# Opening four PSUM banks with a bias product, and reordering the first loads, in a two-layer network kernel

## The reference

```
h     = silu(noise_encoding(t) @ W1 + b1) @ W2 + b2          # t: one number per sequence
scale, shift = h @ Wsc + bsc, h @ Wsh + bsh
out   = silu(scale * LN(x) * gamma + beta ... + shift)       # LN over all 512 x 512 values of a sequence
out   = out @ W_in + b_in
out   = silu(scale * LN(out) ... + shift)
x2    = out @ W_out + b_out + x
r     = gelu(x2 @ Wi[e] + bi[e]) @ Wo[e] + bo[e] + x2        # e: one of 8 experts per sequence, hidden size 2048
y     = LN over channels (r) * gamma[e] + beta[e]
```

## Time and profile before

| | us |
|---|---|
| median of 3 runs (1773.46 to 1773.72) | 1773.62 |
| the profiled execution, own time | 1773.89 |
| its span | 1772.1 |

### The profile page before, as it was taken

One profiled execution on the slowest core, in us unless ns is written; L12 is line 12 of the kernel. 1 busy time (PEld: TensorE's weight loads), 2 busy tenths in 40 slices (PEclk: granted clock), 3 DMA queues, 4 the chain that ended last, 5 costly groups with the idle time before them and its releaser, 6 DMA issues.

```text
span 1772.1 us, 22301 instructions
## 1 busy us (share of the span) xinstructions
PE 1763.0 (99%) x7940; PEld 1454.7 (82%) x7940; DVE 1286.6 (73%) x2147; ACT 976.4 (55%) x1551; POOL 69.1 (4%) x138
## 2 busy tenths in 40 slices
PE   9999999999999999999999999999999999999998
PEld 6888888888888888888888888888888888888887
DVE  6876777767677777767777677677777777777576
ACT  4756554565545656456564555645556555565442
POOL 1000000000000000000000000000000000000000
PEclk9999999999999999999999999999999999999999
DMA  7332332323333233332332313333143332422321
GB/s 292 99 111 75 99 111 84 136 84 99 110 116 114 75 122 110 99 110 72 122 110 99 113 70 122 112 121 110 52 140 113 99 110 71 145 88 75 114 103 69
DMA packets 51906, 189.35 MB, mean 107 GB/s; under 512 B 10451, under 2 KB 14547, under 8 KB 35284
## 3 DMA queue, kind: packets, MB, share of 16 engines
q1 hardware_dynamic: 43156, 183.96, 29.8%
q10 hardware_dynamic: 8640, 3.97, 2.2%
HBM read 171.10 MB, written 16.81 MB: 106 GB/s over the span
## 4 chain that ended last, share of the span: by engine, by line
PE 98%; DMA 1%; SPq 1%; DVE 0%; issue 0%; ACT 0%; POOL 0%; DVEq 0%
PE out_acc L545 39%; PE hid_ps L545 39%; PE blk_ps L545 18%; DMA affine_sb<-in_affine 1%; SPq L364 1%; PE hid_ps L563 0%; PE blk_ps L563 0%; PE out_acc L590 0%; PE hid_ps L590 0%; PE hid_ps L587 0%; PE hid_ps L586 0%; PE blk_ps L586 0%; PE blk_ps L587 0%; PE blk_ps L590 0%; PE out_acc L586 0%
## 5 line engine op out<-in xcount | busy, mean ns | idle before, releaser
L545 PE MATMUL hid_ps<-x_hi,wi_hi 128*128 128x512 f32 x1020 | 397.1, 389 | 0.0
L545 PE MATMUL hid_ps<-x_hi,wi_lo 128*128 128x512 f32 x1020 | 397.1, 389 | 0.0
L545 PE MATMUL hid_ps<-x_lo,wi_hi 128*128 128x512 f32 x1020 | 397.1, 389 | 0.0
L545 PE MATMUL out_acc<-wo_lo,g_hi 128*128 128x512 f32 x1012 | 394.0, 389 | 0.0
L545 PE MATMUL out_acc<-wo_hi,g_hi 128*128 128x512 f32 x1012 | 394.0, 389 | 0.0
L545 PE MATMUL out_acc<-wo_hi,g_lo 128*128 128x512 f32 x1012 | 394.0, 389 | 0.0
L755 ACT ACTIVATE g_sb<-hid_ps,bi_sb 128x512 f32<-128x512 f32 x256 | 175.8, 687 | 311.2 <-PE hid_ps L545 310.9
L883 DVE TENSOR_TENSOR g_lo<-g_sb,g_hi 128x512 fp32r<-128x512 f32 x253 | 173.4, 685 | 189.4 <-ACT g_hi L759 187.7
L715 ACT ACTIVATE wo_hi<-stage 128x512 fp32r<-128x512 f32 x253 | 160.1, 633 | 172.5 <-PE out_acc L545 172.5
L545 PEld LDWEIGHTS hid_ps<-x_hi,wi_hi 128*128 128x128 f32 x1020 | 191.5, 188 | 39.9 <-DVE wi_lo L883 0.2
L545 PEld LDWEIGHTS hid_ps<-x_lo,wi_hi 128*128 128x128 f32 x1020 | 191.5, 188 | 39.6
(11 more groups left out here) (172 smaller groups left out, 1647.7 us busy)
## 6 DMA issues: line engine op xcount, KB each, us to landing
stage<-in_expert_w SPq DMA_DIRECT2D x128, 1024.0 KB, 4.9
x<-in_xT SPq DMA_DIRECT2D x15, 1024.0 KB, 7.3
out_y<-r_sb SPq DMA_DIRECT2D x15, 1024.0 KB, 5.1
rows<-in_expert_rows SPq DMA_DIRECT2D x16, 512.0 KB, 6.8
mv_all<-mv_dram ACTq DMA_DIRECT2D x30, 128.0 KB, 4.4
stage<-in_cond_w SPq DMA_DIRECT2D x4, 512.0 KB, 9.9
affine_sb<-in_affine SPq DMA_DIRECT2D x3, 512.0 KB, 10.2
x<-in_xT SPq DMA_DIRECT2D x4, 256.0 KB, 4.0
```

The costliest lines, as they stand in the source:

```text
L545: last = pe.matmul(dst, w[wp], xs[xp], start=start and i == 0, stop=stop and i == 2)
```

## The change

- SyncE no longer issues the head table and bias_rows: ScalarE's queue does, as its first two instructions. SyncE's order becomes x chunks 0 and 1, W1, x chunks 2 and 3, then as before.
- bias_rows gets b_in as a fourth part (8 KB in place of 6 KB, still one row).
- New `with_bias(m)`: a plain fp32 product of the row b_in (1 x 128) with a row of ones (1 x 512) that opens bank m of layer 1; `first_chunk(0, ...)` then adds onto it. With b_in in the banks, the addition into `bn`, its semaphore and `mean_less` go.
- TensorE's head: 9 products of zeros ahead of the sine in place of 7; `with_bias(0)` and `(1)`, then b2, then 2 zeros products after three statistics, in place of 9 zeros products; `with_bias(2)` in place of 2; `with_bias(3)` in place of 4; the second average is moved ahead of the W2 products; `scale_shift_bias(1)` stands between the W2 halves.
- VectorE: the turn of the W1 product is moved behind the four statistics and their aggregation; `h_lo_part(0, 0, 2)` is moved ahead of `affine(0, 0, 3)`.
- Other banks for the first average, the W1 and the W2 product.

```diff
...
@@ -238,14 +237,14 @@
 
         w1_raw = g_sb[:, 0, :]
         t_sb, cc, small_sb = head_sb[:, 0:B], head_sb[:, B:B + 3], head_sb[:, B + 3:]
-        b_in = small_sb[:, BIN:BIN + DC]
         w2_raw = stage[:, 0].rearrange("p a b n -> p (a b) n")
 
         def cond_raw(m):
             return stage[:, 1 + m // 2, m % 2].rearrange("p h (c n) -> p (h c) n", n=2 * P)
 
 
-        b2_row, bcond_row = (x_sb[1][0:1, a:b, :].rearrange("p c n -> p (c n)") for a, b in ((0, 1), (1, 3)))
+        b2_row, bcond_row, b_in_row = (x_sb[1][0:1, a:b, :].rearrange("p c n -> p (c n)")
+                                       for a, b in ((0, 1), (1, 3), (3, 4)))
         ones = rows[0:1, 0, :]
 
         w_raw = [r_sb, x2_turned]
...
@@ -348,8 +347,8 @@
             return cond_bank[m] if which else out_acc[m]
 
         cond_bank = hid_ps + blk_ps
-        stat_bank = [out_acc[0], blk_ps[1]]
-        m1_bank, m2_bank = out_acc[2], out_acc[3]
+        stat_bank = [blk_ps[1], blk_ps[1]]
+        m1_bank, m2_bank = hid_ps[1], blk_ps[0]
 
         def half(t, h):
 
@@ -372,11 +371,10 @@
             def load_w_in(c):
                 load(w_raw[0][:, c, :], W_in[c * P:(c + 1) * P, :], ld_w_in[c])
 
-            load(head_sb[:, :], head, ld_head)
-            load(w1_raw, W1, ld_w1)
             for c in range(DC):
                 load(x_sb[0][:, c, :], xT[0, c * P:(c + 1) * P, :], ld_first[c])
-            load(x_sb[1][0:1, 0:3, :].rearrange("p c n -> p (c n)"), bias_rows, ld_bias)
+                if c == 1:
+                    load(w1_raw, W1, ld_w1)
             for h in range(2):
                 load(half(w2_raw, h), W2[h], ld_w2[h])
             load_cond(0)
@@ -511,33 +509,41 @@
                     last = strips(m2_bank, m1[:, k, :], of_w(w2_raw[:, k, :]), P, stop=(k == DC - 1))
                 return last
 
+            def with_bias(m):
+
+                pe.matmul(block_bank(0, 0, m)[:, :], b_in_row[:, m * P:(m + 1) * P], ones,
+                          start=True, stop=False)
+
             pe.wait_ge(s_zero, 1)
-            keep_warm(hid_ps[0], 7)
+            keep_warm(hid_ps[0], 9)
             pe.wait_ge(ld_w1, 16)
             pe.wait_ge(s_pad, 1)
             pe.wait_ge(s_sin, 1)
             strips(m1_bank, enc_sin[:, :], of_w(w1_raw), P, start=True, stop=True).then_inc(s_mm1, 1)
-            keep_warm(hid_ps[0], 9)
             pe.wait_ge(s_ones, 1)
             pe.wait_ge(ld_bias, 16)
+            with_bias(0)
+            with_bias(1)
             strips(m2_bank, ones[:, 0:BLOCK], of_w(b2_row), P, start=True)
+            pe.wait_ge(s_bn, DC - 1)
+            keep_warm(hid_ps[0], 2)
             pe.wait_ge(s_average, 1)
             pe.wait_ge(s_mv, 1)
             average_of(0, 0, mv[:, 0, 0:1])
-            keep_warm(out_acc[1], 2)
+            with_bias(2)
+            pe.wait_ge(s_sq, 1)
+            average_of(0, 1, dev[:, 0, 1:2])
             pe.wait_ge(s_pad, 2)
             pe.wait_ge(s_m1, DC)
             w2_half(0)
-            keep_warm(out_acc[1], 2)
-            pe.wait_ge(s_sq, 1)
-            average_of(0, 1, dev[:, 0, 1:2])
+            scale_shift_bias(1)
             w2_half(1).then_inc(s_mm2, 1)
             scale_shift_bias(0)
             pe.wait_ge(s_m2, 1)
             scale_shift(0)
-            for c in range(1, DC):
-                scale_shift_bias(c)
-            keep_warm(out_acc[1], 4)
+            scale_shift_bias(2)
+            scale_shift_bias(3)
+            with_bias(3)
 
             def three(dst, w, xs, start=False, stop=False):
 
@@ -561,7 +567,7 @@
                     else:
                         pe.wait_ge(s_silu, DC * which + 1)
                 pe.matmul(block_bank(0, which, m)[:, HALVES[n]], w_raw[which][:, 0, m * P:(m + 1) * P],
-                          work[:, 0, HALVES[n]], start=(n == 0), stop=False)
+                          work[:, 0, HALVES[n]], start=(bool(which) and n == 0), stop=False)
 
             def first_products(which, m, c):
 
@@ -718,6 +724,8 @@
 
                 act.activation(table_use[:, :], cc[:, 0:1], function)
 
+            act.dma_start(head_sb[:, :], head).then_inc(ld_head, 16)
+            act.dma_start(x_sb[1][0:1, :, :].rearrange("p c n -> p (c n)"), bias_rows).then_inc(ld_bias, 16)
             act.wait_ge(s_enc, 8)
             act.activation(enc_sin[:, 0:B], enc[:, 3, :], ACT.Sin).then_inc(s_sin, 1)
             load_table(ACT.Silu)
@@ -902,11 +910,6 @@
                 dve.bn_stats(bn[:, m, :], src).then_inc(s_bn, 1)
                 if m == DC - 1:
                     dve.wait_ge(s_bn, DC * (turn + 1))
-                    if (b, which) == (0, 1):
-                        means = bn[:, :, 1:6:3]
-                        dve.tensor_tensor(means, means, b_in.unsqueeze(2).to_broadcast([P, DC, 2]), ALU.add) \
-                           .then_inc(s_bnbias, 1)
-                        dve.wait_ge(s_bnbias, 1)
                     dve.bn_aggr(mv[:, which, :], bn[:, :, :]).then_inc(s_mv, 1)
 
             def totals(b, which):
@@ -926,11 +929,7 @@
                 dve.wait_ge(s_avg, 2 * which + 1)
                 dve.tensor_tensor(dev[:, which, 0:1], mv[:, which, 0:1], bank[:, 0:1], ALU.subtract) \
                    .then_inc(s_dev, 1)
-                if which:
-                    dve.tensor_tensor(mean_less[:, :], bank[:, 0:1].to_broadcast([P, DC]), b_in, ALU.subtract) \
-                       .then_inc(s_mean0, 1)
-                else:
-                    dve.tensor_copy(mean(0, which), bank[:, 0:1]).then_inc(s_mean0, 1)
+                dve.tensor_copy(mean(0, which), bank[:, 0:1]).then_inc(s_mean0, 1)
                 dve.wait_ge(s_dev, which + 1)
                 dve.scalar_tensor_tensor(out=dev[:, which, 1:2], in0=dev[:, which, 0:1],
                                          scalar=dev[:, which, 0:1], in1=mv[:, which, 1:2],
@@ -957,7 +956,7 @@
                 else:
                     src = (work if which else x_sb[b % 2])[:, c, :]
                 dve.scalar_tensor_tensor(out=as_affine(work[:, c, :], c), in0=as_affine(src, c),
-                                         scalar=mean_less[:, c:c + 1] if (b, which) == (0, 1) else mean(b, which),
+                                         scalar=mean(b, which),
                                          in1=affine_of(0, c), op0=ALU.subtract, op1=ALU.mult) \
                    .then_inc(s_cen, 1)
 
@@ -975,11 +974,11 @@
                 dve.wait_ge(s_mean0, which + 1)
                 if which:
                     dve.wait_ge(s_hlo, splits_before(turn_of(0, 1)))
-                    src, less = block_bank(0, 0, 0)[:, cols], mean_less[:, 0:1]
+                    src = block_bank(0, 0, 0)[:, cols]
                 else:
                     dve.wait_ge(ld_affine0[n], 16)
-                    src, less = x_sb[0][:, 0, cols], mean(0, 0)
-                dve.scalar_tensor_tensor(out=work[:, 0, cols], in0=src, scalar=less, in1=affine_half(0, n),
+                    src = x_sb[0][:, 0, cols]
+                dve.scalar_tensor_tensor(out=work[:, 0, cols], in0=src, scalar=mean(0, which), in1=affine_half(0, n),
                                          op0=ALU.subtract, op1=ALU.mult).then_inc(s_cen if n else s_cenhalf, 1)
 
             def first_affine(which, n):
@@ -1129,10 +1128,10 @@
                 dve.transpose(cond_sb[:, c].rearrange("p k r -> p (k r)"), cond_bank[c][:, 0:2 * BLOCK]) \
                    .then_inc(s_cond, 1)
 
+            for m in range(DC):
+                stats(0, 0, m)
             dve.wait_ge(s_mm1, 1)
             dve.transpose(m1_raw[:, :, :].rearrange("p c r -> p (c r)"), m1_bank[:, 0:P]).then_inc(s_m1turn, 1)
-            for m in range(DC):
-                stats(0, 0, m)
             first_mean(0)
             first_var(0)
             dve.wait_ge(s_mm2, 1)
@@ -1152,8 +1151,8 @@
             cond_turn(2)
             w_lo_part(0, 2, 2, split_cols(0, 2))
             centre(0, 0, 3)
+            h_lo_part(0, 0, 2)
             affine(0, 0, 3)
-            h_lo_part(0, 0, 2)
             cond_turn(3)
             w_lo_part(0, 3, 3, split_cols(0, 3))
             h_lo_part(0, 0, 3)
@@ -1341,7 +1340,7 @@
         "cond_w": np.stack([A["Wsc"], A["Wsh"]]).reshape(2, DC, P, DC, P // BLOCK, BLOCK)
                     .transpose(3, 2, 1, 4, 0, 5).reshape(DC, P, 2 * DC * P),
         "bias_rows": np.concatenate([A["b2"], np.stack([A["bsc"], A["bsh"]])
-                                     .reshape(2, DC, P // BLOCK, BLOCK).transpose(1, 2, 0, 3).reshape(-1)])
+                                     .reshape(2, DC, P // BLOCK, BLOCK).transpose(1, 2, 0, 3).reshape(-1), A["b_in"]])
                        .reshape(1, -1),
         "affine0": np.stack([A["gamma"].T, A["beta"].T])[:, :P].reshape(2, P, 2, S // 2).transpose(2, 1, 0, 3)
                      .reshape(2, P, S),
```

More of the change, by code:

```diff
@@ L219, in build @@
         bn = sb("bn", [P, DC, 6])
-        mean_less = sb("mean_less", [P, DC])
         mv = sb("mv", [P, 2, 2])
@@ L285, in build @@
```

(2 more changed lines are left out.)

## The result

| | us | ratio to before |
|---|---|---|
| before, median of 7 (1773.37 to 1774.09) | 1773.62 | |
| changed kernel, median of 7 (1778.55 to 1780.80) | 1778.81 | 1.0033, interval 1.0023 to 1.0043 |
| its profiled execution, own time and span | 1778.55, 1776.8 | |

The change made the kernel 5.2 us slower. The forecast was 1772.5, a gain of 1.1, in a range of 1771.6 to 1773.6, with 0.97 on a change within 0.2%; what happened is the third rival, which had 0.04, and half of that for a loss beyond 0.2%.

The account below looks back on a forecast made before the run. The head ahead of layer 2 was taken to decide the time, first through the landing of its loads. Terms of 0.45 (loads), 0.45 (swap) and 0.20 (bias addition) sum to 1.10 us: 1773.62 to 1772.5, range 1771.6 to 1773.6.

Parts of the forecast that it names:

- Rival 3: One-row opening products on TensorE don't keep the higher clock: 1775.3 us, or 1779 with the first chunk doubled; chance 0.04.
- TensorE up to the W2 product: TensorE's head reckoned product by product, 0.95 us per with_bias; first chunk's products start at about 14.5 us, as before.
- Loads, 0.45: First large load issued 0.45 us earlier, so all late landings and chunk 1 come 0.45 earlier; bounds 0 and 0.83.
- Swap, 0.45: Chunk 2's rest part ahead of chunk 3's scaling on VectorE spares TensorE a wait: 0.45 us, bounds 0.29 and 0.5.
- Bias addition, 0.20: Dropping the addition of b_in to VectorE's last statistics and a semaphore step takes 0.20 us off the chain to layer 2.
- W1's product at 5.65: W1, now the third load, lands at 5.65 us, and its product on TensorE runs from 5.65 to 6.05.
- rival 4: ScalarE's DMAs are issued behind its table load, so the head table lands 1.3 us later: 1772.7 to 1772.9; chance 0.12.
- Rival 2: Issue decides the loads: landings 0.83 us earlier, of which 0.54 counts at chunk 1; 1772.3 us; chance 0.08.

Follow-up runs that it names:

- e1: The kernel before, with its zeros products between 5 and 14 us of the head on one row in place of 128: 1780.07 us, ratio 1.0030.
- e2: The changed kernel with its bias products streamed over 128 rows, b_in in row 0 and zeros in the other rows: 1772.80 us, ratio 0.9998.
- e6: The kernel before, with its zeros products between 5 and 14 us of the head on 32 rows in place of 128: 1780.19 us.
- e3: The changed kernel with 128-row zeros products in place of its bias products, b_in added to the statistics again: 1772.98 us, ratio 0.9996.
- e4: The kernel before with only chunk 2's rest part moved ahead of chunk 3's scaling on VectorE: 1773.03 us, ratio 0.9995.
- e8: The changed kernel with 128-row bias products and the head table issued by SyncE again, ahead of x: 1772.98 us, ratio 0.9999.

## Why the prediction was wrong

**The step that failed** is in the working of TensorE up to the W2 product: a with_bias product was priced by its length alone, 0.95 us each, and the zeros products that it replaced were taken as filling. The lengths were right (1.98 for two). But the zeros products had a function that no wait and no chain shows: their 128 rows kept TensorE at 2.4 GHz while the rest of the head gives it only small work. Rival 3 named the mechanism and priced it at 1775.3, or 1779 with the first chunk doubled as well, and 1778.8 was measured. It got 0.04 for the wrong reason: "each was put in place of zeros products that the view shows only as filling" was counted against it, when it was the strongest point for it. A product of zeros whose result nobody reads has no purpose in the computation, which left the clock as the likely one, and e1 shows that it was. What took their place differed in rows and in type; the trace had no one-row product of 512 columns, and e1 and e2 show that the rows were what counted.

The rule that I cited there, from the Trainium skill's "TensorE: Matmul & The Clock Gate", Part 2, that a product's time is set by the columns streamed and not by its rows, agrees with the runs (1.98 us with 1 row and with 128). Part 1 of that page of the Trainium skill says that the clock is set by how busy the engine has been recently. Read as the busy time of the profile, the changed kernel's trace contradicts it: busy for 3.46 of 3.5 us, and the clock fell. The Trainium skill's same page, in the table of "Why this matters for your kernels", says that a single product of 32 rows takes the same time as one of 128; e6's nine of 0.47 us each, the length of a 128-row one at the low level, agree.

The prediction also held that the trace of the kernel before shows nothing for rows either way. For the length it did, in strips of 128 columns, four products each (128 rows, then one row):

```profile
4.71 0.43 PE L470 MATMUL out_acc<-g_sb,enc_sin 128*32 128x128 f32 x8
8.01 0.42 PE L470 MATMUL out_acc<-x,rows 1*32 1x128 f32 x8 [0.60 <-DMA x<-in_bias_rows]
```

**The other steps.**

- *Loads, 0.45:* not confirmed. e3 has the new load order and the swap and gives 1772.98, e4 the swap alone and 1773.03. The landing of W_in's chunk 1 varies more than the term: ScalarE's rounding behind it began at 18.23 in the profiled execution of before and at 17.26 in that of e4, with the same loads in the same order. A term of 0.45 from one execution was within that scatter:

```profile
17.26 0.42 ACT L715 ACTIVATE w_hi<-r_sb 128x256 fp32r<-128x256 f32 x1 [1.87 <-DMA r_sb<-in_W_in]
```

- *Swap, 0.45:* right in mechanism, and e4's 0.65 is in size what was forecast, within its interval.
- *Bias addition, 0.20:* e2 against e3 is 0.18, same sign and size, too small to be shown alone. Swap and addition together gave about 0.52 behind the start of chunk 1, by the changed kernel against e1 (forecast 0.65).
- *W1's product at 5.65:* it came at 6.04, since the sine was late with the head table (5.67 to 5.89); W1 itself had landed at 5.0 (issued at 1.72, 3.3 us). The prediction's "the sine isn't needed until W1 is there" left the table's landing out of the sum. Of rival 4 the symptom was right and the cause not: ScalarE issued both DMAs ahead of its table load, and it was the landing that took 3.0 us in place of 1.7.
- *Rival 2's sum:* 0.54, 0.45 and 0.20 off 1773.62 give 1772.4, not 1772.3.
- *Sum of the rest:* with the clock held, e2 measures 1772.80 against the forecast of 1772.5 for a change without a clock loss, inside the range. That is no support for the loads: swap and addition alone, 0.65 and 0.18, make up nearly all of e2's 0.88. Nearly the whole error is one term: 1778.81 - 1772.80 = 6.0 us.

The lowest medians are those of e2, e3, e8 and e4, 1772.8 to 1773.0. They beat the changed kernel by some 6 us; against the kernel before they are 0.6 to 0.9 lower, which no interval here separates from nothing. e4, the swap alone, is one moved line and had no execution above 1773.41, while e2 had four near 1774.6.

## What to carry to other kernels

Before a filling product on TensorE is replaced by something useful, compare every property of the two, rows and columns as well as length: an engine that is busy throughout can still lose half its clock. In such a place, a one-row product can be written over all 128 rows with zeros in the rest, which took the same time here and was worth 6.0 us. And a rival that one reading can't exclude, and whose price is up to five times the forecast gain, deserves more than 4 in 100.

## What was not expected of the hardware

- In this head TensorE's granted clock depends on how many rows of the array the products use, though their length doesn't: with 1, 32 or 64 rows in 17 filling products the kernel lost 6.0 to 6.6 us (1779.6 to 1780.2), with 128 nothing, and with 96 it lost in three executions of ten. Zeros are enough: the filling is zeros times zeros, and in e2 127 rows of the weights are zeros.
- The clock's record can say 1.00 while the engine runs at the 1.2 GHz level: it has 1.00 from the start in every kernel here, although the first products of 512 columns take 0.47 us each, and in e6 up to about 24.5 us. The length of a known product is the surer sign.
- A 15.5 KB table issued by a second engine beside 256 KB loads took 3.0 us to land, against 1.7 us when it was the first on the only queue (3.0 again in e2, 1.8 in e4 and e8).
